# Int8 layer of a gated cross-attention stack: rows scaled in groups of four tiles on ScalarE, context norms later, last rounding step on GpSimd

## What is computed

```python
def _act_quant(x):
    scale = 127.0 / jnp.clip(jnp.max(jnp.abs(x), axis=-1, keepdims=True), 1e-05)
    xq = jnp.clip(jnp.round(x * scale), -128.0, 127.0) / scale
    return x + jax.lax.stop_gradient(xq - x)
def _bitlinear(x, w):
    return jnp.einsum('bsi,oi->bso', _act_quant(x), _weight_quant(w))
...
h = silu(_bitlinear(xn, w_gate)) * _bitlinear(xn, w_up)     # 512 wide
x = x + jnp.tanh(g_ffn[0]) * _bitlinear(h, w_down)          # xn is x normalised by row
...
```

## Time and profile before

| what | value |
|---|---|
| median of 3 runs | 877.82 us (877.34 to 879.37) |
| the profiled execution's own time | 876.44 us |
| its span, first to last instruction | 874.5 us |
| busy: PE, DVE, ACT, POOL | 605.7, 549.1, 354.5, 242.7 us |
| chain that ended last, by engine | PE 51%, DVE 21%, POOL 7%, issue 7%, ACT 5%, DMA 3% |

### The profile page before, as it was taken

One profiled execution on the slowest core, in us unless ns is written; L12 is line 12 of the kernel. 1 busy time (PEld: TensorE's weight loads), 2 busy tenths in 40 slices (PEclk: granted clock), 3 DMA queues, 4 the chain that ended last, 5 costly groups with the idle time before them and its releaser, 6 DMA issues.

```text
span 874.5 us, 17943 instructions
## 1 busy us (share of the span) xinstructions
PE 605.7 (69%) x5443; PEld 472.7 (54%) x5446; DVE 549.1 (63%) x2108; ACT 354.5 (41%) x896; POOL 242.7 (28%) x285
## 2 busy tenths in 40 slices
PE   1963747877999986998510299916998562299990
PEld 0741326756999974665410288804665452188870
DVE  4887986878677775888650166645888550055552
ACT  0653747832444433555200155503565221144440
POOL 4610000000000004442027455534442017434442
PEclk9985657957999996999855599966999755599996
DMA  5133023000000000000001222250000043222214
GB/s 147 27 117 170 1 67 94 1 7 7 19 24 18 18 0 1 3 2 4 1 14 56 58 72 76 60 158 1 3 3 2 1 113 104 57 53 60 61 40 154
DMA packets 47756, 40.97 MB, mean 47 GB/s; under 512 B 12350, under 2 KB 42332, under 8 KB 47420
## 3 DMA queue, kind: packets, MB, share of 16 engines
q1 hardware_dynamic: 43132, 30.41, 12.2%
q0 software_dynamic: 4544, 9.54, 3.2%
HBM read 23.95 MB, written 15.98 MB: 46 GB/s over the span
## 4 chain that ended last, share of the span: by engine, by line
PE 51%; DVE 21%; POOL 7%; issue 7%; ACT 5%; DMA 3%; SPq 0%; DVEq 0%; ACTq 0%; POOLq 0%
PE ps L1490 10%; PE ps L1060 7%; POOL expert_rows L1559 7%; PE ps L1500 5%; DVE rinvT L479 3%; PE ps L1510 2%; PE ps L653 2%; PE ps L715 2%; PE ps L644 2%; ACT probT L575 2%; PE ps L670 2%; PE ps L1010 2%; PE ps L1079 2%; PE ps L1077 2%; PE ps L1078 2%
## 5 line engine op out<-in xcount | busy, mean ns | idle before, releaser
L1564 POOL DMA_INDIRECT expert_results<-space,b_to x78 | 74.6, 957 | 106.3 <-DVE b_to L1371 101.5
L568 POOL TENSOR_SCALAR xn<-x,moments,rstd 128x128 f32<-128x128 f32 x32 | 25.4, 793 | 278.1 <-DVE rstd L559 278.1
L1490 PE MATMUL ps<-w_block,space 128*128 x312 | 99.9, 444 | 0.0
L1217 DVE SCALAR_TENSOR_TENSOR x<-ps,ew,x 128x128 f32<-128x128 f32 x272 | 76.4, 343 | 28.1 <-PE ps L1060 24.9
L1559 POOL DMA_INDIRECT expert_rows<-sent,slot x64 | 61.7, 963 | 102.2 <-DVE slot L1353 83.3
L1375 DVE TENSOR_TENSOR space<-sg,ps 128x256 f32<-128x256 f32 (+1 forms) x78 | 36.8, 471 | 68.1 <-ACT sg L1430 66.7
L1474 PE MATMUL ps<-const,space 128*128 128x128 f32 x78 | 22.7, 291 | 79.1 <-DMA space<-expert_rows 78.0
L1060 PE MATMUL ps<-w_dn,space 128*128 128x128 f32 x544 | 73.7, 284 | 4.5 <-DVE space L1233 4.3
L1060 PEld LDWEIGHTS ps<-w_dn,space 128*128 128x128 f32 x544 | 69.8, 195 | 10.2 <-DVE space L1233 5.3
L1366 DVE SCALAR_TENSOR_TENSOR b_pick<-space,owner_f 128x4 f32<-128x4 f32 x78 | 16.7, 214 | 86.0 <-DMA space<-expert_rows 86.0
L1490 PEld LDWEIGHTS ps<-w_block,space 128*128 128x128 f32 x312 | 54.8, 196 | 15.5 <-issue 1.6
(11 more groups left out here) (262 smaller groups left out, 1533.8 us busy)
## 6 DMA issues: line engine op xcount, KB each, us to landing
expert_rows<-w_block SPq DMA_DIRECT2D x2, 2632.5 KB, 11.2
space<-expert_rows SPq DMA_DIRECT2D x78, 67.5 KB, 1.9
x_split<-expert_results SPq DMA_DIRECT2D x16, 256.0 KB, 5.1
w_block<-in_L_ffn_w_dram SPq DMA_DIRECT2D x2, 1024.0 KB, 7.0
space<-in_L_ffn_w_dram SPq DMA_DIRECT2D x32, 64.0 KB, 1.9
space<-in_L_ffn_W_dram SPq DMA_DIRECT2D x32, 64.0 KB, 2.3
space<-in_L_ffn_W_dram SPq DMA_DIRECT2D x8, 176.0 KB, 2.8
expert_results<-space,b_to POOLq DMA_INDIRECT x78
```

The costliest lines, as they stand in the source:

```text
L1217: last = dve.scalar_tensor_tensor(x[:, t, :], ps[:, BANK_Y[g % 2], P * j:P * j + P], ew[:, t, bass.ds(n.n, 1)], x[:, t, :], ALU.mult, ALU.add)
L1490: last = pe.matmul(ps[:, bank[s % 2], 0:W], b_xT[:, s % 2, :], w_up[:, bass.ds(expert[s], 1), W * k:W * k + W].rearrange("p a n -> p (a n) ...
L1564: pool.indirect_dma_start(B.results, to, b_y[:, b % 4, :], None).then_inc(y_stored[b % 4], 16)
```

## The change

DVE computes the roots of set 0 only, and then goes through four groups of four tiles. For each group it normalises, reduces, and makes the scale (`xq_asked`). ACT multiplies by the scale and adds `ROUND` (`xq_scaled`), and DVE takes `ROUND` away for the group, after it has normalised the next one. The roots of set 1 come behind the head, before the loop. In the loop the instruction that takes `ROUND` from `hq_t` goes from DVE to POOL, as a function `qff_pool` that POOL runs after `later_pool`.

```diff
-            norm_roots(dve, 0, 1)
-
-            for t in range(TILES):
-                ins = dve.tensor_scalar(xn_all[:, t, :], x[:, t, :], moments[:, 0, t, 0:1], rstd[:, 0, t:t + 1],
-                                        ALU.subtract, ALU.mult)
-            linked_ln(dve, ins)
-            linked_ln(dve, dve.tensor_reduce(q_top[:, 0, :], xn_all[:, :, :], AX.X, ALU.max, apply_absolute_value=True))
-            linked_ln(dve, dve.tensor_scalar(q_top[:, 1, :], q_top[:, 0, :], EPS, 1.0 / 127.0, ALU.max, ALU.mult))
-            linked_ln(dve, dve.reciprocal(q_top[:, 2, :], q_top[:, 1, :]))
-            for t in range(TILES):
-                ins = dve.tensor_scalar(xn_all[:, t, :], xn_all[:, t, :], q_top[:, 2, t:t + 1], ROUND, ALU.mult, ALU.add)
-            linked_ln(dve, ins)
+            norm_roots(dve, 0)
+
+            def normalise(g):
+                some = slice(4 * g, 4 * g + 4)
+                for t in range(4 * g, 4 * g + 4):
+                    ins = dve.tensor_scalar(xn_all[:, t, :], x[:, t, :], moments[:, 0, t, 0:1], rstd[:, 0, t:t + 1],
+                                            ALU.subtract, ALU.mult)
+                linked_ln(dve, ins)
+                linked_ln(dve, dve.tensor_reduce(q_top[:, 0, some], xn_all[:, some, :], AX.X, ALU.max, apply_absolute_value=True))
+                linked_ln(dve, dve.tensor_scalar(q_top[:, 1, some], q_top[:, 0, some], EPS, 1.0 / 127.0, ALU.max, ALU.mult))
+                dve.reciprocal(q_top[:, 2, some], q_top[:, 1, some]).then_inc(xq_asked, 1)
+
+            def quantise(g):
+                dve.wait_ge(xq_scaled, g + 1)
+                dve.tensor_scalar(xq[:, 4 * g:4 * g + 4, :], xn_all[:, 4 * g:4 * g + 4, :], -ROUND, None, ALU.add).then_inc(xq_ready, 1)
             for g in range(4):
-                dve.tensor_scalar(xq[:, 4 * g:4 * g + 4, :], xn_all[:, 4 * g:4 * g + 4, :], -ROUND, None, ALU.add).then_inc(xq_ready, 1)
+                normalise(g)
+                if g:
+                    quantise(g - 1)
+            quantise(3)
...
             ins.then_inc(q_gu_ready, 1)
+            norm_roots(dve, 1)
...
-                if (i := at(3)) is not None:
-                    r = i.par
-                    dve.wait_ge(hq_scaled, i.t + 1)
-                    free_again(dve, hq_turned, 0, i, 2)
-                    dve.tensor_scalar(hq[:, r, :], hq_t[:, r, :], -ROUND, None, ALU.add).then_inc(hq_ready, 1)
...
+        def qff_pool(pool):
+
+            def body(at):
+                if (i := at(3)) is not None:
+                    r = i.par
+                    pool.wait_ge(hq_scaled, i.t + 1)
+                    free_again(pool, hq_turned, 0, i, 2)
+                    pool.tensor_scalar(hq[:, r, :], hq_t[:, r, :], -ROUND, None, ALU.add).then_inc(hq_ready, 1)
+            tile_steps(pool, body, QFF_DEPTH)
...
         def qff_scalar(act):
 
+            def scale(g):
+                act.wait_ge(xq_asked, g + 1)
+                for t in range(4 * g, 4 * g + 4):
+                    ins = act.activation(xn_all[:, t, :], xn_all[:, t, :], ACT.Identity, bias=round_col[:, 0:1], scale=q_top[:, 2, t:t + 1])
+                ins.then_inc(xq_scaled, 1)
+            scale(0)
             for g in range(4):
+                if g < 3:
+                    scale(g + 1)
                 act.wait_ge(xq_turned, g + 1)
...
             later_pool(pool)
+            qff_pool(pool)
```

More of the change, by code:

```diff
@@ L259, in build @@
         q_down = sem("q_down")
+        xq_asked, xq_scaled = sem("xq_asked"), sem("xq_scaled")
         xq_ready, xq_turned, xq_copied = sem("xq_ready"), sem("xq_turned"), sem("xq_copied")
```

## The result

| | before | after |
|---|---|---|
| median, same chip | 874.52 us (20 runs, 870.19 to 880.77) | 869.64 us (20 runs, 865.44 to 877.44 and one of 1959.43) |
| profiled execution, its span | 876.44, 874.5 us | 869.54, 866.7 us |
| the layer in the trace | 59.62 to 125.66: 66.04 us | 59.39 to 119.82: 60.43 us |
| its head, to the first `hid` of DVE | 22.18 us | 21.25 us |
| its loop, from there to the next roots | 43.86 us | 39.18 us |

The ratio of the times is 0.9937, with an interval of [0.9915, 0.996]: the changed kernel is faster by 5.5 us, between 3.5 and 7.4. (The ratio leaves out the one disturbed run of 1959.43 us.) The medians lie 4.9 us apart, inside that interval. The three runs shown before the prediction were 877 to 879 us; with seventeen more on the same chip the median of the same kernel is 3.3 us lower.

What follows compares the result with a forecast made beforehand. DVE was taken to set the loop's step and to work alone in the head. Gains of 1.6 us in the head and 4.3 in the loop, 5.9 in all, took 877.82 to 871.9 us, range 869.2 to 875.2.

Steps and rivals of the forecast that it cites:

- the median 877.82 becomes 871.9: Whole program: 1.6 us from the head and 4.3 from the loop, 5.9 in all, taken off the median.
- I take 0.8: Head: POOL's MEMSET delays DVE's first normalising instruction by 0.8 us, between bounds of 0 and 0.84.
- the change moves neither: Head: the load's arrival and POOL's MEMSET, 62.57 to 64.37, keep their times after the change.
- The bound of 0.84: Head: largest hold by the MEMSET, with the first normalising instruction ending at 64.45 against 63.34 + 0.27.
- The last scaling: Head: ACT's scaling of the last group is not covered by DVE's work, 1.6 us with a hand-over.
- The context's roots: Between head and loop: 3.72 us on DVE, hidden in its idle 5.17 with 0.6 in hand, costed at nothing.
- The slot of 0.33: Loop: DVE loses line 827's slot; fourteen of 16 stand before the last `hid`, 4.6 us gained.
- The last tile: Loop's end: nothing hides POOL's rounding there, 0.3 us lost, with bounds of 0 and 1.1.
- No hold: Rival, head: the MEMSET does not hold DVE's normalising; gain 6.7 us, time 871.1, chance 0.25.
- POOL sets the step: Rival, loop: POOL's rounding and hand-over exceed 2.2 us; time 872.6 at 2.01, 877.2 at 2.4; chance 0.10.
- POOL holds DVE's small instructions: Rival, loop: one-column tensor_scalar is held to POOL's end, step 2.87 us; 3.2 slower, 881.0, chance 0.10.
- It should move up whole: Behind the layer: everything starts from the layer's last row, so all later stages come earlier by the layer's gain.

Runs made afterwards that it cites:

- e3: Changed kernel with POOL's MEMSET moved ahead of its wait for the late loads, beside the first attention: layer 59.09 us, ratio 0.9897 to the kernel before.
- e4: Changed kernel with the context's roots back in front of the head, MEMSET left in place: layer 60.18 us, median 867.37 us (one run).
- e1: Changed kernel with the loop's rounding back on DVE, new head kept: layer 65.03 us, ratio 0.9955 to the kernel before.
- e8: Changed kernel with POOL's rounding done twice, first into an unused buffer: layer 73.45 us, median 881.04 us (one run).
- e7: Changed kernel with a second POOL rounding of 128 columns into an unused buffer each step: layer 60.63 us, median 868.00 us (one run).
- e9: Changed kernel with the MEMSET in POOL's setup and DVE's statistics of tiles 0 to 10 moved near the loop's end: layer 58.34 us, ratio 0.9878.

## Why the prediction came out as it did

**The sum was right, the base was not.** The forecast was 5.9 us of gain. The layer lost 5.61, and the ratio says 5.5 with 5.9 inside its interval. The failed step is in "the median 877.82 becomes 871.9": 877.82 was the median of three runs, and the same kernel's median on that chip is 874.52 over twenty. The step beside it, "the runs before lie within 2.0 us of each other, so I allow 1 us either way", fell as well: twenty runs lie 10.6 us apart. A right gain was set on a base 3.3 us too high, and the time came out 2.3 below the forecast; counted from 874.52, the forecast 871.9 is a gain of 2.6 us only, where 5.5 was measured. The kernel's medians beside the experiments, 876.07 to 877.05, lie below 877.82 too, by 0.8 to 1.8. In the runs of after the span and the granted clock go together for the most part (863.8 us at 0.830, 875.3 at 0.814, but also 872.4 at 0.828), so three runs near each other may all lie on one side. That the gain came so close is in part luck: the head gave 0.7 less than forecast and the loop 0.4 more, and the two misses leave 0.3.

**Head: 0.93 against 1.6.** To the weight load, where the sum counts, it is 0.97 (18.00 against 18.97). Of the terms of the sum the hold by the MEMSET was mis-sized, "I take 0.8": it measured 1.43, and 1.34 when e3 took it away. The mechanism was the one described, to the 0.08 us between POOL's end and DVE's. The size hung on where the MEMSET begins, "the change moves neither": it starts when a load lands, and did so 0.6 later here; over the kernels with it in that place its start ran from 62.57 to 63.70. The bound of 0.84 was made for a fixed place, and was no bound. The remaining terms nearly cancel. The groups took 9.29 from 63.11 to 73.83 less the hold, against 9.42. The last scaling took 1.80 to DVE's rounding at 75.63, against 1.6. Rounding to weight load took 1.76, against 1.85.

**The context's roots: right.** They were over at 79.91 (79.74 and 0.17), and DVE waited 0.72 for the first SiLU; 0.6 was the reserve forecast. That they are hidden is not yet a gain: with the MEMSET in its place e4 is no slower.

**Loop: 4.68 against 4.3.** The slot of 0.33 came back in full, steps 2.20. From the first `hid` to the last it is 31.91 against 36.69: 4.8 where 4.6 was forecast. The last tile lost 0.1, not 0.3.

**POOL: right.** 1.49 us each in all sixteen, against 1.50. The Trainium skill ("GPSIMD Engine Reference", introduction) has VectorE roughly twice as fast at such work; by the rows it was 3.5 times, 1.49 against DVE's 0.42 in e1. A slower engine won all the same, because it was idle.

**The rivals.** "No hold" did not come: 1.93 us for one instruction. "POOL sets the step" did not come at 1.49; e8 shows that it does at 2.98, and e7 that at 2.02 it does not. "POOL holds DVE's small instructions" did not come, and e8 excludes it. The Trainium skill ("SBUF — State Buffer", "Who interferes with whom") says that tensor_scalar can take the port pair shared with GpSimd and that whoever comes second is blocked for the whole instruction. The 128-column instruction beside the MEMSET was blocked to its end, though by the record it began 0.05 before the MEMSET, which is not the page's order; the one-column form was not blocked beside POOL's tensor_scalar.

**"It should move up whole": open to 2 us.** The ratio's gain of 5.5 agrees with the layer's 5.61, but its interval is 3.9 us wide, and what comes behind has two lengths of its own.

## What to carry to other kernels

A forecast of a small gain needs a base that is measured more closely than the gain; three runs that agree need not be near the median. Before moving work into a stretch where another engine was silent or alone, list what starts there on a load's arrival, and give its start a spread of its own: here a MEMSET that nobody waited for ate 1.4 us of a head, and moving it into the setup gave them back to the layer (59.05 against 60.43), though the ratios are too wide to show it for the whole program. An idle slow engine is a good place for a short instruction as long as its duration and hand-overs fit in the new step, and an instruction that lies under another's latency is worth less than its slot when it goes.

## What the runs showed of the hardware

- A POOL MEMSET of 128x2048 f32 (1.80 us) holds a DVE tensor_scalar of 128x128 f32 until 0.08 us after its end: 1.85 us in e3, 1.93 in after, against 0.33 free.
- A DVE tensor_scalar of one column was never held beside POOL's tensor_scalar: 135 to 155 ns in sixteen of sixteen (e8), with POOL busy nearly throughout.
- Behind a reduction of 0.69 us an instruction that needs its result starts at 0.72 (e9), one that doesn't at 0.60 (after). A statistics slot of 0.20 there cost 0.07 to 0.08.
- One stretch of PE work has two lengths, 23.8 to 24.2 and 26.7 us, with granted clocks of 0.67 to 0.69 and 0.57 to 0.62, in kernels that do the same there.
- The loop, which DVE fills, lasts as long at a granted clock of PE of 0.50 (e1, 43.77 us) as at 0.64 (before, 43.86).
